# First stage of a four-layer graph network: adjacency by half tiles, with projections between them

## The reference, cut to what matters

```python
h = jnp.maximum(_layernorm(x, axis=-1), 0.0)          # x: (3327, 256) f32
g = (h @ W_lin.T).reshape(n, 8, 32)
el = jnp.einsum('nhd,d->nh', g, a_l)
er = jnp.einsum('nhd,d->nh', g, a_r)
e = el[:, None, :] + er[None, :, :]                   # per head, all pairs
e = jnp.where(e >= 0, e, 0.2 * e)
e = jnp.where((adj_mat == 0)[:, :, None], -jnp.inf, e)  # adj: (3327, 3327) int32
a = jax.nn.softmax(e, axis=1)
x = x + jnp.einsum('ijh,jhf->ihf', a, g).reshape(n, 256)
```

## Time and profile before

| what | us |
|---|---|
| median of 3 runs (2208.99 to 2215.06) | 2209.24 |
| the profiled execution | 2210.15 |
| its span (first to last instruction) | 2208.4 |

### The profile page before, as it was taken

How to read it: one execution, slowest core, us unless ns; L and a number is a source line. 1 busy time by engine, 2 the same in 40 slices (tenths; PEclk the granted TensorE clock), 3 DMA queues, 4 the chain that set the end, 5 groups by cost and what they waited for, 6 DMA issues and landing times. The chain is left out here.

```text
span 2208.4 us, 58755 instructions
## 1 busy us (share of the span) xinstructions
PE 1979.8 (90%) x23674; PEld 1552.3 (70%) x23674; DVE 1877.9 (85%) x4155; ACT 1607.4 (73%) x1914; POOL 914.7 (41%) x952
## 2 busy tenths in 40 slices
PE   4748999999995899999887999999999999977999
PEld 4548999999994788888654666666666666655544
DVE  5587999999997899988668999999999999985222
ACT  4557999999994776552266999999999999885100
POOL 0020000000005434446316888888888888860000
PEclk9958999999998899999898999999999999997999
DMA  9798221221201156679564212222122211101222
GB/s 306 288 367 308 75 90 57 75 89 55 95 22 41 54 147 160 156 164 190 124 177 144 71 38 69 71 71 70 37 71 71 71 65 42 40 7 48 81 81 71
DMA packets 178078, 235.13 MB, mean 106 GB/s; under 512 B 112195, under 2 KB 143971, under 8 KB 174481
## 3 DMA queue, kind: packets, MB, share of 16 engines
q1 hardware_dynamic: 153408, 203.68, 30.1%
q10 hardware_dynamic: 24400, 27.70, 3.8%
HBM read 161.79 MB, written 49.00 MB: 95 GB/s over the span
## 5 line engine op out<-in xcount | busy, mean ns | idle before, releaser
L2200 DVE CUSTOM_DVE_ANT_0 h_S<-h_ps,off 128x832 f32<-128x832 f32 x832 | 800.1, 1019 | 17.4 <-PE h_ps L2099 16.3
L2099 PE MATMUL h_ps<-KS,QS 98*128 98x416 f16 x1664 | 441.5, 347 | 74.4 <-DVE h_mx L2200 43.0
L2159 ACT ACTIVATE h_H<-h_S,h_nmx 128x2048 fp8e4<-128x2048 f32 x208 | 416.7, 2003 | 69.7 <-DVE h_nmx L2206 69.7
L844 ACT ACTIVATE b_CA<-room,HC 128x1152 fp8e4<-128x1152 f32 (+1 forms) x384 | 435.5, 1219 | 0.0
L945 PE MATMUL b_pb<-xb,room 128*128 128x132 f16 x5408 | 415.8, 222 | 3.6 <-DVE room L906 3.2
L945 PEld LDWEIGHTS b_pb<-xb,room 128*128 128x128 fp8e4 x5408 | 341.9, 97 | 6.5 <-DVE room L906 6.0
L2053 POOL TENSOR_SCALAR h_gap<-h_S,h_nmx 128x1280 f32<-128x1280 f32 x208 | 277.1, 1332 | 91.2 <-DVE h_nmx L2206 81.6
L2058 POOL TENSOR_SCALAR h_H<-h_gap 128x1280 uint8<-128x1280 f32 x208 | 260.5, 1253 | 17.2
L926 PE MATMUL b_pz<-xb,adjT 128*128 128x134 f16 x2704 | 258.1, 222 | 4.3 <-PEq L306 4.3
L2130 PEld LDWEIGHTS h_po<-Vhl,h_HT 128*128 128x128 fp8e4 x5408 | 214.8, 98 | 64.9 <-ACT h_HT L2166 0.7
L2099 PEld LDWEIGHTS h_ps<-KS,QS 98*128 98x128 f16 x1664 | 95.8, 97 | 192.9 <-DVE h_mx L2200 119.0
(11 more groups left out here) (246 smaller groups left out, 3192.0 us busy)
## 6 DMA issues: line engine op xcount, KB each, us to landing
h_rows<-in_adj_dram SPq DMA_DIRECT2D x24, 1663.5 KB, 7.4
room<-in_adj_dram SPq DMA_DIRECT2D x25, 832.0 KB, 6.6
room<-in_adj_dram SPq DMA_DIRECT2D x25, 831.5 KB, 7.5
e_dram<-c_U ACTq DMA_DIRECT2D x78, 256.0 KB, 3.1
xb<-xv_dram SPq DMA_DIRECT2D x44, 435.5 KB, 5.1
adjT_dram<-adjT SPq DMA_DIRECT2D x1, 10816.0 KB, 32.2
c_ad<-adjT_dram SPq DMA_DIRECT2D x13, 832.0 KB, 6.8
m_ad<-adjT_dram SPq DMA_DIRECT2D x13, 832.0 KB, 4.5
```

What stands on the lines that cost most here:

```text
L844: nc.scalar.activation(dst[:, 0:cols], elr[:, n % 2, 0:cols], ACT.Sigmoid, bias=HC[:, h, 1, jt:jt + 1], scale=STEP, saturate=False).then_i ...
L2099: last = nc.tensor.matmul(ps[:, ch % 2, b, 0:SB], QS[:, i % 2, h, :], KS[:, h, c0:c0 + SB], start=True, stop=True)
L2159: nc.scalar.activation(H[:, g % 2, 0:CA], S[:, g % 2, 0:CA], ACT.Exp, bias=nmx[:, g % 2:g % 2 + 1], scale=1.0, saturate=False).then_inc(s_ ...
L2200: nc.vector.tensor_tensor_reduce(out=two(S[:, g % 2, ch * SW:(ch + 1) * SW]), in0=ps[:, ch % 2, :, 0:SB], in1=two(off[:, i % 2, ch * SW:(c ...
```

## The change

The items ("adj", a) become half tiles ("adj", (a, f)), and `startup_order` deals the 52 halves out in another way: two halves, the weights, four halves; then, for each group, one behind the turn, one behind each product and one behind `left`. 48 halves (24 tiles) then stand ahead of `scale`, and the last four behind the first four factors. SP loads tiles 0 and 1 ahead of the second part of X, and the weight matrix ahead of them. DVE takes the statistics of X's second part, `measure(1)`, in the item "turn 0", behind the low part of group 0; the first of the small operations goes with it and the other six go into "turn 1", ahead of the low part of group 1. ACT's root of the second part stands behind `high(0)`. No operation is added or left out.

```diff
 def startup_order():
-    order = [("adj", 0), ("weights", 0), ("adj", 1), ("adj", 2)]
-    a = 3
+    halves = [("adj", (a, f)) for a in range(NT) for f in range(2)]
+    take = lambda n: [halves.pop(0) for _ in range(min(n, len(halves)))]
+    order = take(2) + [("weights", 0)] + take(4)
     for g in range(NGROUPS + 1):
         if g < NGROUPS:
             order.append(("turn", g))
-        order.append(("adj", a))
+        order += take(1)
         if g:
-            order += [("project", t) for t in range(GROUP * (g - 1), min(GROUP * (g - 1) + 2, NT))]
-        if g % 2:
-            order.append(("adj", a + 1))
-        if g:
-            order += [("project", t) for t in range(GROUP * (g - 1) + 2, min(GROUP * g, NT))]
-            order.append(("left", g - 1))
-        a += 1 + g % 2
+            for t in range(GROUP * (g - 1), min(GROUP * g, NT)):
+                order += [("project", t)] + take(1)
+            order += [("left", g - 1)] + take(1)
+        else:
+            order += take(1)
     order.append(("scale", 0))
-    rest = NT - a
     for n in range(len(FACTORS)):
-        while a < NT and (a - (NT - rest)) * len(FACTORS) <= n * rest:
-            order.append(("adj", a))
-            a += 1
-        order.append(("factor", n))
-    return order + [("adj", x) for x in range(a, NT)]
+        order += [("factor", n)] + take(1)
+    return order + halves
...
         def _(sp):
+            load_x(0, s_xa)
+            sp.dma_start(raw, w_lin.rearrange("(k p) c -> p k c", p=P)).then_inc(s_w, 16)
+            sp.wait_ge(s_corner, 1)
+            for a in range(2):
                 for f in range(2):
+                    load(a, f)
+            load_x(1, s_xb)
             sp.wait_ge(s_zero, 1)
...
-            load(0)
-            load(1)
             for kind, i in order:
-                if kind == "adj" and i + 2 < NT:
-                    load(i + 2)
+                if kind == "adj" and i[0] + 2 < NT:
+                    load(i[0] + 2, i[1])
...
         def _(act):
+            root(0)
...
                     high(i)
+                    if i == 0:
+                        root(1)
...
         def _(dve):
+            measure(0)
             for n in range(COUNTED - 1):
-                factors(1, n)
+                factors(0, n)
...
                 elif kind == "turn":
+                    if i == 1:
+                        for n in range(1, COUNTED - 1):
+                            factors(1, n)
                     cn = CHUNKS[i][1]
                     for kc in range(KC):
                         dve.wait_ge(s_hi, 1 + 2 * i + kc + 1)
                         nc.vector.scalar_tensor_tensor(hT[:, i % 2, 1, kc, 0:cn], pt[:, kc, 0:cn], HSC, hT[:, i % 2, 0, kc, 0:cn],
                                                        ALU.mult, ALU.subtract).then_inc(s_lo, 1)
+                    if i == 0:
+                        measure(1)
+                        factors(1, 0)
```

More of the change, by code:

```diff
@@ L340, in _, with load, load_x @@
         def _(sp):
-            def load(a):
+            def load(a, f):
                 s, t = a % 2, TILES_IN[a]
-                for f in range(2):
[L344 to L352, removed]
+                c0, c1 = f * HC1, (N if f else HC1)
+                if a >= 2:
+                    sp.wait_ge(s_atr[f], a - 1)
+                for p0, p1 in (LAST_CUTS if t == NT - 1 else ((0, P),)):
+                    sp.dma_start(rows[p0:p1, s, c0:c1], adj_dram[t * P + p0:t * P + p1, c0:c1]).then_inc(s_rows[s][f], 16)
+            def load_x(half, done):
+                t0, t1 = halves[half][0], min(halves[half][1], NT - 1)
+                sp.dma_start(k.X[:, t0:t1, :], x_dram[t0 * P:t1 * P, :].rearrange("(t p) d -> p t d", p=P)).then_inc(done, 16)
+            load_x(0, s_xa)
+            sp.dma_start(raw, w_lin.rearrange("(k p) c -> p k c", p=P)).then_inc(s_w, 16)
+            sp.wait_ge(s_corner, 1)
+            for a in range(2):
+                for f in range(2):
+                    load(a, f)
+            load_x(1, s_xb)
             sp.wait_ge(s_zero, 1)
@@ L355, in _ @@
                 sp.dma_start(k.X[p0:p1, NT - 1, :], x_dram[(NT - 1) * P + p0:(NT - 1) * P + p1, :]).then_inc(s_xb, 16)
-            sp.dma_start(raw, w_lin.rearrange("(k p) c -> p k c", p=P)).then_inc(s_w, 16)
-            sp.wait_ge(s_corner, 1)
-            load(0)
-            load(1)
             for kind, i in order:
-                if kind == "adj" and i + 2 < NT:
-                    load(i + 2)
+                if kind == "adj" and i[0] + 2 < NT:
+                    load(i[0] + 2, i[1])
             for f in range(2):
@@ L400, in _, with transposes @@
         def _(pe):
-            def transposes(a):
-                t = TILES_IN[a]
+            def transposes(a, f):
                 if a == 0:
                     pe.wait_ge(s_id, 3)
[L405 to L414, removed]
+                landed(pe, a, f)
+                if a == 2 and f == 1:
+                    pe.wait_ge(s_pad, 3)
+                if a:
+                    pe.wait_ge(s_aev[f], a)
+                for n in range(HALF):
+                    j0 = (f * HALF + n) * P
+                    last = nc.tensor.transpose(tr[:, f, n * P:(n + 1) * P], low16[:, a % 2, j0:j0 + P, 0], k.ident16[:])
+                last.then_inc(s_atr[f], 1)
             def weights():
@@ L466, in _ @@
                 if kind == "adj":
-                    transposes(i)
+                    transposes(*i)
                 elif kind == "weights":
@@ L484, in _, with root @@
                                   attn_w[side * HD:(side + 1) * HD].rearrange("(p o) -> p o", o=1)).then_inc(s_at, 16)
-            for half, (t0, t1) in enumerate(halves):
+            def root(half):
+                t0, t1 = halves[half]
                 act.wait_ge(s_sm, COUNTED * half + 2)
                 nc.scalar.activation(sm[:, 1, t0:t1], sm[:, 0, t0:t1], ACT.Sqrt).then_inc(s_sq, 1)
+            root(0)
             def relu(g):
@@ L533, in _ @@
                 if kind == "adj":
-                    act.wait_ge(s_atr[1], i + 1)
-                    nc.scalar.activation(k.adjT[:, TILES_IN[i], HALF:NT, :].rearrange("p j i -> p (j i)").bitcast(U8),
-                                         tr[:, 1, 0:HC1].bitcast(U16), ACT.Copy, scale=float(FP8_ONE)).then_inc(s_aev[1], 1)
+                    a, f = i
+                    if f == 1:
+                        act.wait_ge(s_atr[1], a + 1)
+                        nc.scalar.activation(k.adjT[:, TILES_IN[a], HALF:NT, :].rearrange("p j i -> p (j i)").bitcast(U8),
+                                             tr[:, 1, 0:HC1].bitcast(U16), ACT.Copy, scale=float(FP8_ONE)).then_inc(s_aev[1], 1)
                 elif kind == "weights":
@@ L606, in factors, with measure @@
                 ins.then_inc(s_sm, 1)
-            for half, (t0, t1) in enumerate(halves):
+            def measure(half):
+                t0, t1 = halves[half]
                 dve.wait_ge(*((s_xb, 48) if half else (s_xa, 16)))
@@ L611, in _ @@
                     nc.vector.bn_stats(stats[:, t, :], k.X[:, t, :]).then_inc(s_stat, 1)
-                    if half and t - t0 < COUNTED - 1:
-                        factors(0, t - t0)
                 for t in range(t0, t1):
@@ L664, in _ @@
                 if kind == "adj":
-                    dve.wait_ge(s_atr[0], i + 1)
-                    nc.vector.tensor_scalar(k.adjT[:, TILES_IN[i], 0:HALF, :].rearrange("p j i -> p (j i)").bitcast(U8),
-                                            tr[:, 0, 0:HC1].bitcast(U16), float(FP8_ONE), None, ALU.mult).then_inc(s_aev[0], 1)
+                    a, f = i
+                    if f == 0:
+                        dve.wait_ge(s_atr[0], a + 1)
+                        nc.vector.tensor_scalar(k.adjT[:, TILES_IN[a], 0:HALF, :].rearrange("p j i -> p (j i)").bitcast(U8),
+                                                tr[:, 0, 0:HC1].bitcast(U16), float(FP8_ONE), None, ALU.mult).then_inc(s_aev[0], 1)
                 elif kind == "weights":
```

## The result

The changed kernel takes **2221.7 us** in the median (8 runs, 2216.96 to 2228.9) against 2209.84 for the kernel before on the same chip: a ratio of **1.0047, 95% interval 1.0035 to 1.0058**. It is slower, by 11.9 us where 8.8 were forecast. The profiled execution took 2219.89 us (span 2218.2), 9.7 more than the 2210.15 of before. The longer executions are those with the lower granted clock of the whole span (2216.96 us at 0.960, 2228.9 us at 0.953). That holds for the kernel before too (on another chip 2206.34 us at 0.961 and 2217.34 at 0.953), so by itself it says nothing of the first stage.

The account below looks back on a forecast made before the run. Factors wait for adjacency while the projection part, chained through three engines, leaves transfer time unused. First factor 144.1 plus factors 39.8 gives 183.9 against 174.9, 9.0 us longer: 2218 us; own range 2213 to 2224, overall 2207 to 2229.

Parts of the forecast that it names:

- Start to turn 0: From kernel start to PE's turn 0, behind tile 2's landing: 33.5 us, before 35.06; bounds 30.5 and 36.5.
- The statistics: X's second-part statistics on DVE behind group 0's low part: DVE away from 39.0 to 46.5 us, delaying PE and ACT.
- The one step ahead of turn 2: PE turns half 0 of tile 5 at 55.5 us, then 6.2 us of its work to turn 2 at 61.7.
- A full group: Between two turns, an evacuation chain through ACT, DVE and PE: 13.5 us, bounds 12.7 and 16.1.
- Turn 6 to the first factor: Last adjacency halves, store and reduction before the factors: 28.4 us, first factor at 144.1, before 117.00.
- Factors: The 16 factors at the first stage's end, DVE and POOL products excluding one another: 39.8 us; bounds 31 and 43.
- the forecast's list of signs: Profile signs of being right, among them turn 2 near 62, first L693 near 144, L661 and L693 means well over 1.04.
- No exclusion: Rival: among the factors DVE and POOL pass one another, 31 us instead of 39.8, total 2209.5 us; chance 0.18.
- Landings set the pace and the statistics hide: Rival: up to turn 6 PE makes up, turn 2 at 54, groups 12.7 us, total 2207 us; chance 0.12.
- It doesn't do what it says: Rival: PE meets the same evacuation waits elsewhere, added semaphore waits cost 0.2 each, group 14.5, total 2222 us; chance 0.06.
- The clock: Rival: PE's 3.2 us wait in every group lowers its clock, group 16.1, +10 us, total 2228 us; chance 0.14.
- the last of the sum: From the profiled execution's forecast 2219.2 us to the median, taken 0.9 lower: 2218 us.

Follow-up runs that it names:

- experiment 4: Changed kernel with ACT's relus of the next turn moved right behind `left`, ahead of the evacuation of the half that follows: 2219.18 us, ratio 1.0027 to the kernel before.
- Experiment 3: Changed kernel with all 16 factor products on DVE and none on POOL: ratio 1.0023 to the kernel before, factors 34.7 us instead of 40.1.
- the second measurement: The changed kernel run again unchanged, beside the version with extra matmuls: 2223.75 us (6 runs), ratio 1.0046 to the kernel before.
- experiment 2: Changed kernel plus 26 unused PE matmuls in the wait of each of six groups: 2217.45 us, ratio 1.0017 to the kernel before; unchanged beside it 2223.75 us.

## Why the prediction was right, point by point

**Start to turn 0.** Forecast 33.5, measured 32.54: transfers in the first 30 us ran at 294 GB/s instead of 267, so tile 2 was there a little sooner, within the bounds given.

**The statistics.** Forecast: DVE away from 39.0 to 46.5. The timeline of the changed kernel:

```profile
38.02 5.97 DVE L615 BATCH_NORM_STATS2 s_stats<-X 128x6 f32<-128x256 f32 x18
43.90 1.28 DVE L618 BATCH_NORM_AGGREGATE s_mv<-s_stats 128x2 f32<-128x6 f32 x18
45.31 1.88 DVE L672 TENSOR_SCALAR adjT<-s_tr 128x1664 uint8<-128x1664 uint16 x1
45.43 0.22 ACT L484 ACTIVATE s_sm<-s_sm 128x18 f32<-128x18 f32 x1 [8.17 <-DVE s_sm L596]
47.34 1.55 PE L409 MATMUL s_tr<-ident,room 128*128 128x128 bf16 x13 [8.52 <-DVE adjT L672]
61.54 1.04 PE L433 MATMUL s_pt<-ident,xb 128*128 128x128 f32 x8
```

18 statistics took 5.97 (6.0) and DVE was away from 38.0 to 45.3; ACT stood for 8.17 us in its root and PE for 8.52, each behind it. This is work that hid in the wait for the first landings and now hides nowhere. The one step ahead of turn 2 came out in two offsetting pieces: half 0 of tile 5 was turned at 54.28, 1.2 sooner than forecast, and from there to turn 2 it took 7.26 us, not 6.2. The granted clock was 0.79 in that stretch: PE's first transposes after standing took 1.55 us for 13, against 0.89 later. The sum had no clock in it there, so that turn 2 was met, 61.54 (61.7), is partly luck.

**A full group.** Forecast 13.5 with a PE wait of 3.2 in one piece, measured 13.36 and 3.37:

```profile
61.54 1.04 PE L433 MATMUL s_pt<-ident,xb 128*128 128x128 f32 x8
...
63.19 2.06 ACT L496 ACTIVATE xb<-X,s_sm 128x256 f32<-128x256 f32 x4
...
66.97 1.88 DVE L672 TENSOR_SCALAR adjT<-s_tr 128x1664 uint8<-128x1664 uint16 x1
68.99 0.38 PE L409 MATMUL s_tr<-ident,room 128*128 128x128 bf16 x4 [3.37 <-DVE adjT L672]
74.90 1.04 PE L433 MATMUL s_pt<-ident,xb 128*128 128x128 f32 x8
```

The second half 0 stands at 7.45 behind the turn (7.3), the rest takes 5.91 (6.2). Compare: there ACT's relus began 0.6 behind the turn, here 1.65, because the half behind `left` is evacuated in front of them. In the groups behind it PE's wait was not in one piece, and a part of it was for landings (1.14 us at 78.52 and 1.16 at 92.79), which the forecast had named as a sign of being wrong; the groups took 13.36 and 13.45 all the same. **A term mis-sized beside it:** I had the transfers at 12.7 us for a group, from a 404 GB/s row, and called them almost the limit and not the cause. They ran at 364 to 402 and needed up to 14.0, so they were as much the limit as the chain (experiment 4). The sum did not show it, as both stand near 13.4.

**Turn 6 to the first factor.** 29.5 us, forecast 28.4. From the last half of adjacency on:

```profile
134.56 0.90 PE L409 MATMUL s_tr<-ident,room 128*128 128x128 bf16 x13 [0.39 <-DMA room<-in_adj_dram]
135.50 1.56 ACT L536 ACTIVATE adjT<-s_tr 128x1664 uint8<-128x1664 uint16 x1 [0.92 <-PE s_tr L409]
135.50 0.62 ACTq L524 DMA_DIRECT2D el_dram<-xb  x2
140.47 0.64 DVE L642 TENSOR_REDUCE s_rm<-s_GE 128x8 f32<-128x208 f32 x1 [5.12 <-DMA el_dram<-xb]
144.60 1.05 DVE L705 TENSOR_TENSOR xb<-s_GE,s_vf 128x858 f32<-128x858 f32 x1
```

The last half before `scale` was turned at 19.5 behind turn 6, not 16.7, and PE waited for its landing. That the transfers had used up their lead, so that the mis-sized rate is behind it, is argued. And 1.5 us that I charged to ACT were not paid: the store was issued at 135.50, as ACT's evacuation began and not as it ended. Two errors of opposite sign, then, of which the sum shows only the difference. Store to reduction 4.97 (5.0), reduction to the first factor 4.13 (4.1).

**Factors.** 40.1, forecast 39.8, with DVE and POOL excluding one another. Experiment 3 shows that POOL is what stretches DVE, 34.7 without it, and the timeline of a pair shows how: one runs behind the other. By the Trainium skill ("GPSIMD Engine Reference", section 1, Specifications) GpSimd contends with VectorE's instructions that have two SBUF inputs; the trace agrees: only L665 is stretched, with two inputs from SBUF, to a mean of 1.64, and the evacuations from PSUM (L672) stay at 1.88. Wrong in the forecast's list of signs: L705 (L693 before) did not stretch, 1.04 in the mean. DVE's product is always the one that POOL waits behind, so the low parts carry it all; the sum is the same.

**The rivals.** *No exclusion* falls with experiment 3. *Landings set the pace and the statistics hide*: no, PE stood 8.52 us behind the statistics; but its first half was near the truth in the groups. *It doesn't do what it says*: no, the groups took 13.4 us, not the 14.5 given for it. *The clock* was given as all or nothing, and is a matter of the execution: in the profiled one no full group lost it, and the sum met its 2219.89 within 0.7 us (2219.2), but in others one did, as the second measurement shows (0.89, 14.84 us). Its reason was wrong as well: a wait of 2.69 us, called harmless because the kernel before kept its clock through it, was followed by a loss in another execution (experiment 2). The step that failed is the last of the sum: it took the median 0.9 below the profiled execution, as before, and it lies 1.8 above. These 2.7 us are most of the 3.7 by which the forecast was low; that it was the clock is argued from the runs' clocks, not shown, since those are of the whole span.

## What to carry to other kernels

Work that stands in a wait for the first data is free there; here it cost its full length where it was moved to: moving 7.5 us of statistics out of it cost 7.4 to 7.7 us, or 9.2 in an execution that lost clock besides. When transfers idle in one part and limit another, move tiles only until both limits meet (two a group gave 0.9958 to 0.9969, three gave 1.0047 with the new start and 1.0023 with the old, 0.9993 with extra matmuls to hold the clock); the tile after that costs more in front than it saves behind. Before dividing elementwise work between DVE and POOL, look for rows in which both are longer than alone, and try it on one. And before a us or two between two profiles is put down to an edit, compare the stretch ahead of the edit, and the granted clock group by group.

## What the runs showed of the hardware that was not expected

**A DMA issued from ACT's queue does not wait for the operation that ACT is running.** Evacuation and store stand at the same 135.50 above. In the kernel before, there are two stores at this place, of the last two groups. The first of them:

```profile
104.20 1.56 ACT L535 ACTIVATE adjT<-s_tr 128x1664 uint8<-128x1664 uint16 x1 [1.11 <-PE s_tr L413]
104.96 0.27 ACTq L525 DMA_DIRECT2D el_dram<-xb  x1
105.66 0.36 ACT L519 ACTIVATE xb<-s_pg 8x256 f32<-8x256 f32 x1
```

It was issued 0.8 us before the end of the one operation and 0.7 before the start of the other, and both stand ahead of it in ACT's list. The second store, at 106.04, waits for the values of the other operation and came right behind its end.

**The granted clock differs between executions of one kernel.** In the same groups it was 1.00 in one profile of the changed kernel and 0.89 once in another, 1.00 to 0.79 with the old start. A wait of PE of 2.69 us left it at 1.00 in the kernel before and was followed by 0.85 in the variant with the old order; a group lost 1.4 to 2.2 us by it. With 26 short matmuls in each wait all groups stood at 1.00, and the medians were lower by 6.3 us on one chip and by 0.3% (1.0023 to 0.9993) between two, of which only a part is shown to be the groups'.

**The rate of the same adjacency transfers** was 364 GB/s at a share of 0.98 between turns 2 and 3, and 402 to 414 from turn 5 on. Which of the other transfers or addresses makes this is open.

**POOL's first product** began 7.7 us after its reduction across partitions (at 149.91, idle 7.74), 7.21 before, and 9.2 in the variant with the new start and the old order.
